# Two graph-attention layers with expert networks: block numbers loaded sixteen at a time from a plain table, unread semaphore increments taken out, and the load order changed at two stage heads

## The reference

```
h  = layernorm(x)
q, k, v = h @ wq, h @ wk, h @ wv                 # 8 heads of 32
s  = (q[dst] * k[src]).sum(head) + edge_bias      # per edge and head
a  = segment_softmax(s, dst)
x1 = x + segment_sum(a * v[src], dst) @ wo
y  = layernorm(x1); e = argmax(y @ wg)            # one of 8 experts per node
x2 = x1 + gate * expert_e(y)                      # gelu network of expert e
h_r = layernorm(x2) @ w_r                         # for each of the 8 relations r
s, a as before, from h_type[src] and dst
x3 = x2 + segment_sum(a * h_type[src], dst)
out = x3 + top-2 mixture of 8 expert networks of layernorm(x3)
```

## Time and profile before

| | |
|---|---|
| median of 3 runs | 5298.51 us (5294.61 to 5303.6) |
| profiled execution | 5326.32 us, its span 5324.5 us |
| mean granted TensorE clock | 0.894 |
| PE busy | 4280.5 us (80%) |
| DVE busy | 3132.7 us (59%) |
| POOL busy | 2166.5 us (41%) |
| ACT busy | 1838.4 us (35%) |

### The profile page before, as it was taken

The page is one execution under the profiler, slowest core; times in us unless marked ns, Lnnn a source line. Parts: engine busy times, 40 slices in busy tenths (PEclk is TensorE's granted clock), DMA queues, the critical chain, the costliest instruction groups (busy, mean ns, idle before and its releaser), DMA issues. The chain is left out here.

```text
span 5324.5 us, 89607 instructions
## 1 busy us (share of the span) xinstructions
PE 4280.5 (80%) x21797; PEld 3214.9 (60%) x21798; DVE 3132.7 (59%) x8529; ACT 1838.4 (35%) x5242; POOL 2166.5 (41%) x2307
## 2 busy tenths in 40 slices
PE   7577777777776993799999577777777777999999
PEld 4355454544554993799644355555555556878877
DVE  5399999888996442011122166666666665555555
ACT  2244444444441330233233244333333422222222
POOL 4456666655661333000222366666665631111110
PEclk9799999999998995899999687788787888999999
DMA  6555655555552115111244333333333321000000
GB/s 190 162 153 169 169 168 164 161 162 163 167 169 94 39 40 186 55 35 37 104 178 175 127 92 93 90 91 92 91 93 89 94 61 42 16 14 14 16 14 11
DMA packets 231311, 543.03 MB, mean 102 GB/s; under 512 B 46241, under 2 KB 128686, under 8 KB 222158
## 3 DMA queue, kind: packets, MB, share of 16 engines
q0 software_dynamic: 112976, 348.83, 23.7%
q1 hardware_dynamic: 118013, 190.48, 10.3%
HBM read 423.60 MB, written 115.55 MB: 101 GB/s over the span
## 5 line engine op out<-in xcount | busy, mean ns | idle before, releaser
L277 POOL DMA_INDIRECT attn_KV<-kv_tab,attn_stage x832 | 866.5, 1042 | 560.6 <-issue 343.6
L1820 POOL DMA_INDIRECT rel_V<-h_tab,rel_stage x832 | 830.2, 998 | 570.8 <-issue 243.4
L392 PE MATMUL attn_SP<-attn_KV 128*128 128x264 f32 x1664 | 562.4, 433 | 263.5 <-DVE node L494 174.0
L1920 PE MATMUL rel_SP<-rel_V,rel_OH 128*128 128x264 f32 x1664 | 635.5, 505 | 170.8 <-DVE node L1991 134.7
L392 PEld LDWEIGHTS attn_SP<-attn_KV 128*128 128x128 f32 x1664 | 285.3, 200 | 482.7 <-issue 457.6
L379 PE MATMUL attn_QP<-node,attn_OHT 128*128 x1664 | 505.4, 431 | 45.0 <-issue 28.8
L1920 PEld LDWEIGHTS rel_SP<-rel_V,rel_OH 128*128 128x128 f32 x1664 | 350.0, 240 | 311.2 <-DVE node L1991 182.1
L1991 DVE TENSOR_TENSOR node<-node,rel_SP 128x264 f32 x832 | 351.4, 422 | 259.3 <-PE rel_SP L1920 140.4
L494 DVE SCALAR_TENSOR_TENSOR node<-node,same,attn_SP 128x264 f32 x832 | 397.4, 478 | 114.7 <-PE attn_SP L392 53.7
L2196 ACT ACTIVATE moe_HT<-moe_HB,moe_b 128x128 f32<-128x128 f32 x800 | 228.7, 368 | 670.0 <-PE moe_HB L2213 670.0
L2213 PE MATMUL moe_HB<-moe_YT,moe_W 128*128 128x128 f32 x3200 | 410.5, 283 | 0.0
(11 more groups left out here) (337 smaller groups left out, 6994.6 us busy)
## 6 DMA issues: line engine op xcount, KB each, us to landing
h_tab<-pr_H SPq DMA_DIRECT2D x50, 1056.0 KB
attn_KV<-kv_tab,attn_stage POOLq DMA_INDIRECT x832
rel_V<-h_tab,rel_stage POOLq DMA_INDIRECT x832
kv_tab<-qkv_KV SPq DMA_DIRECT2D x50, 256.0 KB
attn_runs<-runs SPq DMA_DIRECT2D x52, 192.0 KB
rel_runs<-runs SPq DMA_DIRECT2D x52, 192.0 KB
Wd<-in_wd SPq DMA_DIRECT2D x8, 1024.0 KB
y_sorted<-gate_zeros SPq DMA_DIRECT2D x8, 928.0 KB
```

What stands on the lines that cost most here:

```text
L277: pool.indirect_dma_start(out=KV[:, i * IT + u, 0:2 * FEAT], out_offset=None, in_=d["kv_tab"][:, :], in_offset=bass.IndirectOffsetOnAxis(a ...
L392: pe.matmul(SP[u % SUMS][:, 0:NUMC], KV[:, j * IT + u, 0:P], KV[:, j * IT + u, FEAT:ROW], start=True, stop=True).then_inc(s["sums"], 1)
L1820: pool.indirect_dma_start(out=V[:, i * IT + u, :], out_offset=None, in_=d["h_tab"][:, :], in_offset=bass.IndirectOffsetOnAxis(ap=stage[:, ...
L1920: pe.matmul(SP[(j + u) % SUMS][:, 0:NUMC], OH[:, j * IT + u, :], V[:, j * IT + u, :], start=True, stop=True).then_inc(s["sums"], 1)
```

## The change

It has five parts.

1. **Block numbers.** `m.jgroup` (one packed word per period) becomes `m.block_of` (a whole number for each step). `blocks_of` loads sixteen numbers into sixteen registers with one register load, and no register arithmetic follows.
2. **Holds.** The unread increments are dropped in both layers, at the runs loads (SyncE), the gathers (GpSimd), the distances (ScalarE), and on TensorE ahead of every sum of the attention layer and of the `cols` transposes in both. The wait then stands on the instruction behind it.
3. **Tables.** The chain that packs the words goes (three DMAs, five small VectorE operations at t = 14, 17 memsets and their waits). An integer copy `ji`, its store at t = 6 and the load of `block_of` at t = 9 come.
4. **Gate head.** SyncE issues x block 0 first, then Wo on a semaphore of its own, the other five loads, and puts the fills one after each of the iterations t = -2 to 1 and two after t = 2 and 3. PE waits for Wo only, and for the rest at t = 0; DVE waits for the rest at t = 1; ACT waits for the rest as before.
5. **Moe head.** x blocks 0 and 1 go first, then Wr, W1 with b1, and W2 with b2, each on a semaphore of its own. DVE waits for none of them, ACT for W1, PE for Wr at t = -1 and for W1 and W2 at t = 0.

In the sort stage four scratch tiles also become slices of another tile. The diff, cut to its core:

```
         def blocks_of(g, engine):
-            packed = nc.values_load_multi_w_load_instructions(m.jgroup[0:1, bass.ds(g, 1)], engines=[engine],
-                                                              min_val=0, max_val=(PACK << IT) - 1)[1][0]
-            blks = [packed & (PACK - 1)]
-            for u in range(1, IT):
-                blks.append(blks[-1] + ((packed >> (6 + u)) & 1))
-            return [nc.s_assert_within(b, 0, LAST_BLOCK, skip_runtime_bounds_check_because="each is a step's block number")
-                    for b in blks]
+            return nc.values_load_multi_w_load_instructions(m.block_of[0:1, bass.ds(g * IT, IT)], engines=[engine], min_val=0,
+                                                            max_val=LAST_BLOCK, skip_runtime_bounds_check_because="each is a step's "
+                                                            "block number")[1]
...
                             need(pe, s["added"], c * IT + (u + 1 - SUMS))
-                            hold(pe, m)
                             pe.matmul(SP[u % SUMS][:, 0:NUMC], ...
...
     (gate stage, SyncE)
+                def weights():
+                    for k in range(2):
+                        sp.dma_start(Wo[:, k, :], d["wo"][k * P:(k + 1) * P, :]).then_inc(s["wo"], 16)
+                    for k in range(2):
+                        sp.dma_start(W1[:, k, :], d["w1"][k * P:(k + 1) * P, :]).then_inc(s["w"], 16)
+                    ... b1, Wg, bg on s["w"]
...
+                    if isinstance(t, int) and t == -LEAD:
+                        weights()
+                    if isinstance(t, int) and t == -2:
+                        sp.wait_ge(s["zeroed"], 1)
+                    if isinstance(t, int) and -2 <= t < 2:
+                        fill([t + 2])
+                    if isinstance(t, int) and 2 <= t < 4:
+                        fill([2 * t, 2 * t + 1])
...
     (gate stage, TensorE; VectorE has the second wait at t == 1 and the first no more)
-                pe.wait_ge(s["w"], 16 * LOADS)
+                pe.wait_ge(s["wo"], 32)
+                    if isinstance(t, int) and t == 0:
+                        pe.wait_ge(s["w"], 16 * LOADS)
...
     (moe stage: SyncE, ScalarE, TensorE, VectorE)
+                    if isinstance(t, int) and t == 1 - LEAD:
+                        weights()
-                act.wait_ge(s["w"], 16 * LOADS)
+                act.wait_ge(s["w1"], 48)
-                pe.wait_ge(s["w"], 16 * LOADS)
+                    if isinstance(t, int) and t == -1:
+                        pe.wait_ge(s["wr"], 32)
+                    if isinstance(t, int) and t == 0:
+                        pe.wait_ge(s["w1"], 48)
+                        pe.wait_ge(s["w2"], 48)
-                dve.wait_ge(s["w"], 16 * LOADS)
```

More of the change, by code:

```diff
@@ L46 @@
 SORTED += SORTED % 2
-PACK = 64
-assert BLOCKS <= PACK and PACK ** 4 <= 2 ** 24
 QSCALE = float(DH) ** 0.5
@@ L690, in project_with_tables @@
         s = sems(nc, m, "qkv", "w mm q_out kv_out kv_free stored0 stored1")
-        p = sems(nc, m, "prep", "last iota link ends ends_sb less bsel rows jt_turned jt jf jb blocks dst src typ attr sent cleared "
-                 "steps ids powers packed group jg jgroup rawf turned turned_sb ne tail scaled pl links mixed masked out")
+        p = sems(nc, m, "prep", "last iota link ends ends_sb less bsel rows jt_turned jt jf jb dst src typ attr sent cleared "
+                 "steps ids block_of rawf turned turned_sb ne tail scaled pl links mixed masked out")
         x_in = [new_sem(nc, m, f"qkv_x_in{i}") for i in range(2)]
@@ L733, in project_with_tables @@
         attr = pb("attr", [P, SGROUPS, HEADS * P], F32)
-        blocks = pb("blocks", [GROUPS, IT + 1], F32)
-        moves = pb("moves", [GROUPS, IT], F32)
-        powers = pb("powers", [GROUPS, IT], F32)
-        total = pb("total", [GROUPS, 1], F32)
-        total_i = pb("total_i", [GROUPS, 1], I32)
+        ji = pb("ji", [SGROUPS, P], I32)
         pt = ctx.enter_context(nc.psum_tensor("prep_pt", [P, 2, 512], F32))
@@ L753, in tables @@
                     if t == 6:
-                        sp.wait_ge(p["jt"], 1)
+                        sp.wait_ge(p["jt"], 2)
                         sp.dma_start(d["jf"][:, :], jt[:, :]).then_inc(p["jf"], 16)
+                        sp.dma_start(d["ji"][:, :], ji[:, :]).then_inc(p["jf"], 16)
                     if t == 9:
-                        sp.wait_ge(p["jf"], 16)
+                        sp.wait_ge(p["jf"], 32)
+                        sp.dma_start(m.block_of[0:1, :], d["ji"].rearrange("k p -> (k p)")[0:SPAD].rearrange("(o s) -> o s", o=1)
+                                     ).then_inc(p["block_of"], 16)
                         sp.dma_start(jb[:, :], steps[0:SPAD].rearrange("(o s) -> o s", o=1).to_broadcast([P, SPAD])).then_inc(p["jb"], 16)
-                    if t == 10:
-                        sp.wait_ge(p["cleared"], 2)
-                        by_group = steps[IT - 1:IT - 1 + (GROUPS - 1) * IT].rearrange("(g s) -> g s", s=IT)
-                        with nc.allow_non_contiguous_dma(reason="block numbers by group, and the one before each group"):
-                            sp.dma_start(blocks[:, 1:IT + 1], steps[0:SPAD].rearrange("(g s) -> g s", s=IT)).then_inc(p["blocks"], 16)
-                            sp.dma_start(blocks[1:GROUPS, 0:1], by_group[:, 0:1]).then_inc(p["blocks"], 16)
                     if t == 11:
@@ L1010, in _ @@
                 dve.memset(ids[:, FULL, :], 0).then_inc(p["cleared"], 1)
-                dve.memset(blocks[0:1, 0:1], 0.0).then_inc(p["cleared"], 1)
                 dve.memset(m.same[:, 0:1], 0.0)
-                for u in range(IT):
-                    dve.memset(powers[:, u:u + 1], float(PACK << u)).then_inc(p["powers"], 1)
                 for t in iterations:
@@ L1310, in sort_by_expert @@
         AB = sb("AB", [P, 2, 2 * HEADS], F32)
-        hot = sb("hot", [P, BE], F32)
-        pick = sb("pick", [P, BE], F32)
-        sums = [sb(f"sums{i}", [P, BE], F32) for i in range(2)]
+        hot = m.sd[:, 0:BE]
+        pick = m.sd[:, BE:2 * BE]
+        sums = [m.sd[:, (2 + i) * BE:(3 + i) * BE] for i in range(2)]
         top = sb("top", [P, BLOCKS], F32)
```

77 lines of the change are left out of this document (26 added, 51 removed).

## The result

The changed kernel takes 5099.56 us (median of 4, 5097.1 to 5118.2) beside 5296.56 us before: ratio 0.9641, interval 0.9607 to 0.9674. That is 197 us less. I forecast 42 to 45 us less and a range whose low end was 5195; the direction was right, the size was not, and the measured time lies outside the range.

The account below looks back on a forecast made before the run. VectorE paces attention, a TensorE-VectorE loop the relational layer, TensorE the gate stage. Terms -9 - 11.5 - 17.5 - 5 - 1.5 = -44.5 us gave 5281.8 profiled, 5254 as median; range 5195 to 5460.

Parts of the forecast that it names:

- the price of the layers' waits: Both layers: each exposed VectorE wait gains 0.09 us, two ALU operations; attention taken as 0.18 us a period, -9 us.
- four exposed gaps a period: Relational layer: four waits ahead of VectorE's adds each lose 0.09 us of ALU operations, -0.36 us a period.
- The holds: Both layers: TensorE's unread increments priced at nothing extra; 10 us more if all 0.051 us showed at 194 waits.
- t16: Both layers: time of one sixteen-word register load, taken as 0.90 us, bounds 0.30 and 4.5.
- My relational sum: Relational layer: sixteen-word load time less 1.12 us a period, -0.22 at 0.90, -11.5 us in all.
- L2007's idle time: Relational layer, VectorE's "issue" idle: from 1.08 us a period to 1.4; 0.8 or over 4 under other load prices.
- The page's rule: Block-number loads: some 200 ns per register even in bulk, so about 3.3 us a load, +158 us, 5456; chance 0.12.
- Heads and tables: Gate head -17.5 us with 2 us for fills, moe head -5 us, table building -1.5 us.
- (a) serial fetch: Both layers: sixteen words fetched one after another, 4.5 us a load, +283 us, 5581; chance 0.22, including 0.12 at 3.3 us.
- (b) burst: Both layers: sixteen words come together, 0.30 us a load, relational -43 us, total -76, 5222; chance 0.27.
- (c) layers unmoved: Both layers: the TensorE and VectorE loop takes back what the queues gain, -24 us, 5274; chance 0.07.
- (d) fills: Gate head: x or `y_tab` queue behind zero fills and eat its gain, about 5290, no change; chance 0.06.

Follow-up runs that it names:

- h_act: Kernel before without ScalarE's holds (4 a period and layer), waits kept: ratio 1.0000 on a fast chip, 0.9993 on a slow one.
- alu_pe: Changed kernel with two register operations put back ahead of each block number's use on TensorE only: 4832.61 us, ratio 0.9924 on a fast chip.
- h_pe: Kernel before without TensorE's holds (17 a period in attention, 1 in relational), waits kept: ratio 1.0010 on a fast chip, 0.9977 on a slow one.
- h_pool: Kernel before without GpSimd's holds (8 a period and layer), waits kept: ratio 1.0003 on a fast chip, 0.9857 on a slow one.

## Why the prediction was wrong, by its steps

- **The step that failed** is the price of the layers' waits: "70 in 44 periods, 1.6 a period, x 0.09 = 0.14 us", and for the relational layer "I count four exposed gaps a period". It took the number of VectorE's waits and the length of what is removed. The rows beside it said that these waits lasted 0.9 us (43.9 us in 48) and 2.1 us (43.7 in 21), far longer than the 0.3 us in which an add follows its sum on the fast chip, on an engine that is busy 90% of the time. I did not ask what made them so long; the change took most of them away in the attention layer. Even where nothing pauses the 0.09 was too low: in the relational layer of the fast chip an add that had to wait starts 0.31 us after its sum's end with the register operations (h_act) and 0.15 without (alu_pe).
- **The holds**, "I count nothing apart from what stands above", rested on one row where TensorE waits for VectorE. The row was misread: half of its 0.11 us was the hold. Where the add ends last, TensorE's weight load starts 0.115 us after it with the hold (h_act) and 0.053 without (h_pe). TensorE's holds carry 12 us (1 to 23; I had named 10 as the bound). The 73 us are GpSimd's, an engine that I did not price at all.
- **t16**: 1.10 measured, 0.90 taken. My relational sum with it, 1.10 - 1.12, gives -1 us for that layer. The sign I named was L2007's idle time, from 1.08 us a period to 1.4; it came to 0.97. The mean of 1.08 hid the stretched operations: the median of that gap was 0.54 us before and is 0.96 after, and on the fast chips it goes from 0.54 (h_pe) to 0.96 (alu_pe), +0.42, near the +0.34 that I had. On the fast chips, where the pauses are absent, the layer went from 1085.6 (h_pe) to 1080.9 (alu_pe), -4.7, and attention from 1253.1 to 1243.8, -9.3, against -9 priced (-6 and -8 beside h_pool and h_act). There alu_pe, with TensorE's register operations still in, comes near all my terms but the relational one: start -3, attention -9, gate -16, relational -5, moe head -4, 37 us by the stretches and 34 by the medians, of 44. That the attention layer's -9 came out there is partly luck, since the 0.09 it was made of was too low and the number of waits was the slow chip's. In the relational layer on the fast chips the reason of the small gain is another one than I gave: GpSimd never has to wait for room in the ring. The gathers of h_act, 2900 to 3900 us:

```profile
L1819 POOL DMA_INDIRECT rel_V<-h_tab,rel_stage x756 | 766.1, 1013 | 230.3 <-issue 198.0 <-PE rel_SP L1918 32.0 <-ACT rel_stage L1829 0.3
```

  The idle time is 0.305 us for each of the 756, the gap that back-to-back gathers have; 16 x (1.013 + 0.305) = 21.1 us, and a period takes 21.05 from gather to gather. The loop of TensorE and VectorE that I read as the bound is not the bound there.
- **The page's rule** of the Trainium skill ("Runtime: NRT & Kernel Launch", "Instruction fetch mechanics", some 200 ns per register) does not hold for this load: 53 ns per further register. Elsewhere the page describes such loads as loads from HBM, and the table lies in SBUF; I should have seen that it need not bear on it.
- **Heads and tables**: right in mechanism and size; the fills cost the gate stage 1 us (19.4 us earlier at block 0's x1, 18.5 at the stage's end), where I took 2.
- **Rivals**: (a) serial fetch, (b) burst, (c) layers unmoved and (d) fills all fell. None said that the layers' stalls themselves would go. The low end of the range, 5195, was built from t16, the moe head and 10 us for the holds.

**Shown and not shown.** Shown: the layers' 199 us split into 80 for the table and 98 for the holds; of the holds' share 73 us are GpSimd's, of the table's some 40 are VectorE's register operations (by an estimate across chips). The parts were found on the slow chips and shrink to 14 us in both layers in the nearest variant on a fast one. The number of DMA completions is not the cause, and the number of increments not the main one. Shown too is what a hold does to the gather behind it, 0.5 us where it waits in full. Not shown: what the pauses of the slow chips are, and why taking away register operations and holds removes most of them in the attention layer. My own explanation, that GpSimd's run of gathers holds up the other engines' semaphores and sequencers, has the layer heads for it and the steady pauses against it, in which GpSimd mostly stands; no run slowed the gathers on a slow chip. Why the chips differ is open.

## What to carry to other kernels

When an engine that sets the pace is idle in waits far longer than the work that they wait for, find out what those waits are before pricing a change by its instructions: their removal can be worth ten times the instructions. Price every engine's blocking semaphore instructions, the gathering engine's first (0.5 us for each gather that waited in full here), and let the wait stand on the instruction that needs it. Take a second chip before generalising: the same change is worth 3.6% on one kind of chip and under 1%, by its nearest variants, on another, and a cost found on one can be zero on the next.

## What the runs showed of the hardware that I had not expected

- A register load of sixteen neighbouring words from SBUF takes 1.10 us on TensorE and on VectorE, one word 0.30.
- A semaphore instruction that blocks ahead of a gather on GpSimd delays a gather that has to wait by 0.5 us: it starts 0.79 us after the sum's end with it, 0.27 without. Ahead of a sum on TensorE it costs 0.06 us (0.115 and 0.053). Its own row shows 0.017 and 0.051 us.
- Chips differ by 9 to 10% on this kernel (4866 us, and 5293 to 5340), nearly all of it in the two layers in which GpSimd gathers: 1253 for 1382 us, 1086 for 1321, and 39 to 44 us at each layer's start. The experts and the moe stage agree to 0.3%.
- On the chips of the slower kind a register operation of 0.045 us now and then takes 0.7 us in the relational layer; on the faster kind none of 1560 takes over 0.051.
- On the chips of the slower kind TensorE, VectorE and ScalarE do a sixth of their work while GpSimd issues 40 gathers in 50 us at a layer's start, at nearly the same DMA rate (120 and 127 GB/s).
